# Cross attention with its running maxima in bf16, and their negatives spread by one product of a constant tile with placed tops

## The chip, the cores and the metric

The kernel runs on one core of one Trainium2 chip. The core's engines are TensorE (PE; its weight loads are shown apart as PEld), VectorE (DVE), ScalarE (ACT), GpSimd (POOL) and SyncE (SP, which only issues transfers here). Each engine works through its own list of instructions in order, and semaphores tie the lists together. The metric is the device time of one execution in microseconds; lower is better.

## The reference, cut to what matters

The program is a two-layer decoder on `x` of shape (4, 256, 256): self attention, memory attention and a ternary feed-forward network, then a gated scan, cross attention and a mixture of experts. The change lies in the cross attention of the second layer. Per batch row there are 256 queries in 16 heads of width 128 and 4 key/value heads, each shared by four query heads; the keys are the 256 own positions and 1601 context positions, 1857 in all:

```
q, k = rope(rms_norm(x @ Wq)), rope(rms_norm(own_and_context @ Wk))
p    = exp((q @ k.T - m) * 128**-0.5)      # m: one number per query and head, near the row's maximum
out  = (p @ v) / sum(p)                    # any m gives the same quotient; it guards against overflow
x   += out @ Wo
```

## The kernel before, in words

Scores are made transposed: keys on the partitions, queries along the free dimension. A **pass** h is one half (two heads x 256 queries = 512 columns) of one of the 16 groups (batch row, key/value head), so there are 32 passes (`PASSES`), two to a group; a pass with an even h is the first half of its group. Each pass has 15 **steps** (`STEPS`), one per tile of 128 keys (65 in the last). `cross_stream` writes the program of every engine by hand as a loop over **slots** (`SLOTS`), one step per slot: in slot s the functions are called that are due at s minus a fixed lag (`TOPS_LATE`, `LOWER`, `WEIGH` and so on). Nothing reorders this afterwards.

For one step: PE makes the scores (`score`, L1956, three bf16 products into bank 0 or 1), ACT copies them to SBUF (`copy_scores`, L2053), DVE takes the running maximum from the bank (`keep_most`, L2237 for the second step of a pass, L2240 for the rest), 18 slots later DVE adds the negative maximum (`lower`, L2226, which reads PSUM bank 7), ACT makes the exponent (L2059), POOL sums it up (L2168) and PE weighs the values (`weigh`, L1988). Beside this PE projects keys, values and queries for a later group (L1899), DVE rotates them (`rotate`, L2281 and L2282), POOL normalises them (L2175, L2181, L2186) and PE turns them (L1941); such a unit comes every five slots. `score` for step s waits until `keep_most` has read the bank at step s - 2.

At the end of a pass comes what is called a **turnover** here, numbered like its pass. The maximum over the partitions of `most` (128 x 512, f32) is taken and brought back to every partition:

- slot 15: `turn_most` (PE, L1964), four f32 transposes of `most` into bank 6
- slot 16: `take_top` (DVE, L2260), the maximum of each row, 128 x 4; `turn_top` (PE, L1970), a bf16 product that turns these to 4 x 128; `flatten` (ACT, L2101), the copy to SBUF as `flat` with its sign changed
- slot 17: `spread` (PE, L1977), four products of the rows of `own` (four rows of an identity, widened to 4 x 4 x 128) with `flat`, which put row c of `flat` on all partitions of bank 7. It waits for `flatten` and for the last `lower` of the pass before (65 x 512), which DVE does in slot 17
- slot 18: the first `lower` of the pass waits for `spread`

(slots counted from the pass's first.) `own` comes from an 8 x 8 constant that a transfer brings in at the start of the cross attention (L1663) and a DVE copy widens (L1695).

Of the kernel before, what the change touches and what calls it, by code (L numbers as in the profile page):

```python
# [8 lines left out]
ALU = mybir.AluOpType  # L9
# [9 lines left out]
P = 128  # L19
# [4 lines left out]
DC = DM // P  # L24
# [1559 lines left out]
TOPS_LATE, FLAT_LATE, SPREAD_LATE = STEPS, STEPS + 1, STEPS + 2  # L1584
# [49 lines left out]
def cross_attention(nc, x, const, a, w, kept, first_row, experts):  # L1634

    with Stage(nc, "cross") as keep:
# [6 lines left out]
        own8 = sb("own8", [8, 8])  # L1643
        own = sb("own", [4, 4, P], BF16)
# [6 lines left out]
        with Stage(nc, "cross_w") as st:  # L1651
# [5 lines left out]
            loaded, dve_step, rs_ready, rs_done, row_ready = (st.sem(s) for s in ("loaded", "dve_step", "rs_ready", "rs_done", "row_ready"))  # L1657
            row_t, own_hi = st.sem("row_t"), st.sem("own_hi")

            with nc.Block() as block:  # L1660
                @block.sync
                def _(sp):
# [27 lines left out]
                def _(ve):  # L1690
# [3 lines left out]
                    ve.wait_ge(loaded, 16)  # L1694
                    nc.vector.tensor_copy(own[:], bcast(own8[0:4, 0:4], 2, P))  # L1695
# [11 lines left out]
        cross_stream(nc, x, const, a, w, experts, w_q, w_kv, w_o, k_gain, q_gain, freq, ones, own, half, eps, own_t, in_t, ctx_t,  # L1707
# [3 lines left out]
def cross_stream(nc, x, const, a, w, experts, w_q, w_kv, w_o, k_gain, q_gain, freq, ones, own, half, eps, own_t, in_t, ctx_t,  # L1711
                 where, where_f, angle, turns, sin, k_tab, q_tab, raw):

    with Stage(nc, "stream") as st:
# [20 lines left out]
        flat = spare[0:4, DC * CTX - 128:DC * CTX - 64].bitcast(BF16)  # L1735
# [11 lines left out]
        most_turned, top_ready, top_turned, flat_ready, spread_ready = (  # L1747
            sem("most_turned"), sem("top_ready"), sem("top_turned"), sem("flat_ready"), sem("spread_ready"))
# [94 lines left out]
        for s in SLOTS:  # L1843
            for kind, items in (("tops", pass_at(s, TOPS_LATE)), ("flat", pass_at(s, FLAT_LATE)), ("turn", turns_in(s)),
                                ("sum", pass_at(s, SUM_LATE)), ("out", outs_in(s))):
                for item in items:
# [3 lines left out]
                    freed = {"tops": lambda: (top_ready, item + 1), "flat": lambda: (flat_ready, item + 1),  # L1850
# [3 lines left out]
        with nc.Block() as block:  # L1854
# [34 lines left out]
            def _(pe):  # L1889
# [131 lines left out]
                for slot in SLOTS:  # L2021
# [7 lines left out]
                    for h in pass_at(slot, FLAT_LATE):  # L2029
                        turn_top(h)  # L2030
# [706 lines left out]
```

## Time and profile before

| what | value |
| --- | --- |
| time, median of 3 runs | 1650.81 us (1650.22 to 1650.82) |
| profiled execution's own time | 1648.11 us |
| its span, first to last instruction | 1646.3 us |
| busy over the span: PE, DVE, ACT, POOL | 89%, 78%, 63%, 69% |
| granted TensorE clock, mean over the span | 0.966 |
| cross attention, steps and tail | from about 459 to 1567 us |

Busy shares are of the whole span and count neither register work nor waits. PE's busy time is modelled: a product of 512 columns is shown with 0.38 us, while the next one starts 0.21 to 0.22 us after it, so starts of consecutive PE rows say what a product costs and not their lengths. Consecutive DVE rows overlap too, by up to 0.09 us. A few PE records are missing.

### The profile page before, as it was taken

Reading aid. Unit: us, or ns where it says so; the run is one execution under the profiler, and the core shown is the slowest. Engines: PE = TensorE matmul, PEld = TensorE weight load, DVE = VectorE, ACT = ScalarE, POOL = GpSimd, SP = SyncE. Lnnn points to the kernel's source line nnn. Section 1 sums busy time; section 2 is a strip of 40 time slices with the busy share of each in tenths; the row PEclk is TensorE's granted clock in tenths of the full one; section 3 lists DMA queues with packets and bytes.
Section 4 is the critical chain, followed back from the end, with each engine's and each line's share of the span. In section 5 each row is a group of like instructions: output and inputs, shape, how many; then the busy total and the mean of one; then the engine's idle time right before and its main releaser. Section 6 shows DMA issues by size and latency. Waiting matters only on the chain. (4 is left out here: it accounts for less than half of the span.)

```text
span 1646.3 us, 25844 instructions
## 1 busy us (share of the span) xinstructions
PE 1470.2 (89%) x8223; PEld 855.8 (52%) x8332; DVE 1287.7 (78%) x2581; ACT 1029.3 (63%) x2439; POOL 1127.9 (69%) x1033
## 2 busy tenths in 40 slices
PE   6598697757778999999999999989999999999988
PEld 5477365533544555455455555545545555554455
DVE  7876577878569888787977888887887878878766
ACT  3364464744366777676677766676776766766552
POOL 2363471112459789988978998888898878877742
PEclk9799798979899999999999999999999999999999
DMA  3000831020000001000000100000000000000020
GB/s 102 1 2 2 296 114 39 1 73 0 32 1 14 14 1 41 14 1 1 1 1 1 28 14 1 1 1 1 14 28 1 1 1 1 1 1 1 1 59 26
DMA packets 30991, 38.47 MB, mean 23 GB/s; under 512 B 4996, under 2 KB 26504, under 8 KB 30856
## 3 DMA queue, kind: packets, MB, share of 16 engines
q1 hardware_dynamic: 30856, 36.82, 6.9%
q8 instruction: 67, 1.10, 0.3%
q14 instruction: 68, 0.56, 0.1%
HBM read 35.76 MB, written 1.05 MB: 22 GB/s over the span
## 5 line engine op out<-in xcount | busy, mean ns | idle before, releaser
L2168 POOL TENSOR_TENSOR stream_acc<-stream_acc,stream_weights 128x512 f32<-128x512 f32 (+1 forms) x374 | 491.9, 1315 | 80.6 <-ACT stream_weights L2059 59.0
L1988 PE MATMUL stream_banks<-stream_weights,stream_v 128*128 128x512 f32 (+1 forms) x876 | 451.6, 600 | 0.0
L2240 DVE TENSOR_TENSOR stream_most<-stream_most,stream_banks 128x512 f32<-128x512 f32 (+1 forms) x416 | 284.9, 685 | 157.4 <-ACT stream_weights L2053 142.2
L2053 ACT COPY stream_weights<-stream_banks 128x512 f32<-128x512 f32 (+1 forms) x438 | 256.6, 586 | 238.8 <-PE stream_banks L1956 231.0
L2059 ACT ACTIVATE stream_weights<-stream_weights 128x512 f32<-128x512 f32 (+1 forms) x438 | 278.5, 637 | 60.2 <-DVE stream_weights L2226 57.6
L2226 DVE TENSOR_TENSOR stream_weights<-stream_weights,stream_banks 128x512 f32<-128x512 f32 (+1 forms) x438 | 297.0, 680 | 2.8 <-PE stream_banks L1977 1.5
L2175 POOL TENSOR_TENSOR stream_by_cos<-stream_by_cos,stream_by_sin 128x256 f32<-128x256 f32 x192 | 135.8, 728 | 88.4 <-DVE stream_by_sin L2282 88.2
L1956 PE MATMUL stream_banks<-stream_q_t_lo,stream_k_t_hi 128*128 128x512 bf16 (+1 forms) x479 | 181.7, 379 | 9.2 <-DVE stream_most L2240 3.1
L1956 PE MATMUL stream_banks<-stream_q_t_hi,stream_k_t_lo 128*128 128x512 bf16 (+1 forms) x480 | 182.1, 379 | 0.1
L1956 PE MATMUL stream_banks<-stream_q_t_hi,stream_k_t_hi 128*128 128x512 bf16 (+1 forms) x388 | 147.6, 381 | 15.5 <-DVE stream_most L2240 14.8
L1988 PEld LDWEIGHTS stream_banks<-stream_weights,stream_v 128*128 128x128 f32 (+1 forms) x876 | 144.0, 191 | 29.7 <-issue 5.3
L1956 PEld LDWEIGHTS stream_banks<-stream_q_t_hi,stream_k_t_hi 128*128 128x128 bf16 (+1 forms) x480 | 47.2, 98 | 140.6 <-issue 99.0
L1956 PEld LDWEIGHTS stream_banks<-stream_q_t_lo,stream_k_t_hi 128*128 128x128 bf16 (+1 forms) x480 | 47.5, 99 | 134.7 <-issue 134.3
L2186 POOL TENSOR_TENSOR stream_normed<-stream_by_cos,row_ctx_t 128x512 f32<-128x512 f32 x96 | 96.8, 1008 | 8.4 <-PE stream_banks L1941 1.1
L2069 ACT ACTIVATE stream_squares<-stream_banks 128x128 bf16<-128x128 f32 x368 | 97.2, 278 | 8.1 <-PE stream_banks L1899 7.8
L2181 POOL TENSOR_TENSOR row_ctx_t<-row_ctx_t,cross_half 128x4 f32<-128x4 f32 x96 | 98.2, 1023 | 0.0
L1899 PE MATMUL stream_banks<-early_w_kv_hi,row_in_t_hi 128*128 128x256 bf16 x416 | 79.4, 273 | 5.0 <-DVE stream_by_sin L2282 5.0
L1899 PE MATMUL stream_banks<-early_w_kv_lo,row_in_t_hi 128*128 128x256 bf16 x416 | 79.4, 273 | 0.0
L1899 PE MATMUL stream_banks<-early_w_kv_hi,row_in_t_lo 128*128 128x256 bf16 x416 | 79.4, 273 | 0.0
L2069 ACT ACTIVATION_READ_ACCUMULATOR stream_squares<-stream_banks 128x1 f32 x368 | 77.1, 210 | 0.0
L1956 PEld LDWEIGHTS stream_banks<-stream_q_t_hi,stream_k_t_lo 128*128 128x128 bf16 (+1 forms) x480 | 47.4, 99 | 56.5 <-issue 0.3
L1899 PEld LDWEIGHTS stream_banks<-early_w_kv_hi,row_in_t_hi 128*128 128x128 bf16 x416 | 40.4, 98 | 51.8 <-DVE stream_by_sin L2282 6.0
(445 smaller groups left out, 3099.6 us busy)
## 6 DMA issues: line engine op xcount, KB each, us to landing
memory_raw_t<-in_ctx_t SPq DMA_DIRECT2D x4, 1601.0 KB, 9.1
memory_raw<-in_ctx SPq DMA_DIRECT2D x4, 1536.0 KB
row_ctx_t<-in_ctx_t SPq DMA_DIRECT2D x6, 512.0 KB, 3.7
early_raw<-in_L_xattn_Wq SPq DMA_DIRECT2D x4, 512.0 KB, 3.8
early_raw<-in_L_xattn_Wo SPq DMA_DIRECT2D x4, 512.0 KB, 3.9
row_ctx_t<-in_ctx_t SPq DMA_DIRECT2D x1, 1601.0 KB, 7.0
moe_raw_up<-in_L_ffn_wi SPq DMA_DIRECT2D x6, 256.0 KB, 4.3
model_x<-in_x SPq DMA_DIRECT2D x1, 1024.0 KB, 5.4
```

Source lines behind the costliest of these rows:

```text
L1899: last = nc.tensor.matmul(out, rows, moving(two, c), start=(n == 0), stop=(n == 3 * DC - 1))
L1956: last = nc.tensor.matmul(ps[0:r, step % 2, :], k_t[one][:, t * P:t * P + r], q_t[two][:, g % 2, PAIR * n:PAIR * (n + 1), :], start=(one = ...
L1988: nc.tensor.matmul(ps[:, 2 + n, :], v[0:r, g % 2, t, :], room(step)[0:r], start=(t == 0), stop=(t == KT - 1)).then_inc(weighed, 1)
L2053: nc.scalar.copy(room(step)[0:r], ps[0:r, step % 2, :]).then_inc(copied, 1)
L2059: nc.scalar.activation(room(step)[0:r], room(step)[0:r], ACT.Exp, scale=SCALE).then_inc(p_ready, 1)
L2069: last = nc.scalar.activation(squares[:, h, :], heads[:, h - some.start, :], ACT.Square, accum_out=ss[:, u % 2, h:h + 1])
L2168: nc.gpsimd.tensor_tensor(acc[0:r, h % 2, :], acc[0:r, h % 2, :], room(step)[0:r], ALU.add).then_inc(acc_ready, 1)
L2175: last = nc.gpsimd.tensor_tensor(by_cos[:, u % 2, 0:n, to], by_cos[:, u % 2, 0:n, to], by_sin[:, u % 2, 0:n, of], ALU.add)
L2181: nc.gpsimd.tensor_tensor(rms[:, u % 2, 0:n], var[:, u % 2, 0:n], half[:, 0:n], ALU.pow).then_inc(rms_ready, 1)
L2186: nc.gpsimd.tensor_tensor(normed[:, 0:n], by_cos[:, u % 2, 0:n], bcast(rms[:, u % 2, 0:n], 2, HD), ALU.mult).then_inc(normed_ready, 1)
L2226: nc.vector.tensor_tensor(room(step)[0:r], room(step)[0:r], ps[0:r, 7, :], ALU.add).then_inc(lowered, 1)
L2240: nc.vector.tensor_tensor(most[0:r], most[0:r], ps[0:r, step % 2, :], ALU.max).then_inc(maxed, 1)
```

## The change

`most` becomes bf16 (each running maximum is rounded), and `turn_most` transposes it as bf16 into the first half of bank 6, seen as bf16 (`turned_most`). `take_top` reads those. `turn_top` and `flatten` are gone. In their place DVE gets `place_top` in slot 16, after `take_top` and `lower` and ahead of `rotate`: it multiplies the bf16 identity with `top`, each read four times and 128 times over, which gives `tops`, four diagonal tiles of 128 x 128 with the tops on the diagonals. `spread` is then a single bf16 product of `less`, a constant 128 x 128 tile of -1.0, with the 512 columns of `tops`; every partition of bank 7 gets the negative tops. It waits for `place_top` instead of `flatten`. The constant's transfer and the copy that widened it are gone; POOL fills `less`.

```diff
         ones = sb("ones", [P, 1])
-        own8 = sb("own8", [8, 8])
-        own = sb("own", [4, 4, P], BF16)
+        less = sb("less", [P, P], BF16)
...
-                    sp.dma_start(own8[:], a["c_cross_own"]).then_inc(loaded, 16)
...
                     nc.gpsimd.memset(ones[:], 1.0)
+                    nc.gpsimd.memset(less[:], -1.0)
...
-                    ve.wait_ge(loaded, 16)
-                    nc.vector.tensor_copy(own[:], bcast(own8[0:4, 0:4], 2, P))
                     ve.wait_ge(rs_done, 1)
...
-        most = sb("most", [P, HALF])
+        most = sb("most", [P, HALF], BF16)
+        tops = sb("tops", [P, 4, P], BF16)
         top = sb("top", [P, 4], BF16)
...
+        turned_most = ps[:, 6, :].bitcast(BF16)[:, 0:HALF]
...
                     for c in range(4):
-                        last = nc.tensor.transpose(ps[:, 6, c * P:(c + 1) * P], most[:, c * P:(c + 1) * P], const["ident"][:])
+                        last = nc.tensor.transpose(turned_most[:, c * P:(c + 1) * P], most[:, c * P:(c + 1) * P], const["ident_b"][:])
                     last.then_inc(most_turned, 1)
 
-                def turn_top(h):
-                    pe.wait_ge(top_ready, h + 1)
-                    wait_bank6("flat", h)
-                    nc.tensor.matmul(ps[0:4, 6, 0:P], top[:], const["ident_b"][:], start=True, stop=True).then_inc(top_turned, 1)
-
                 def spread(h):
-                    pe.wait_ge(flat_ready, h + 1)
+                    pe.wait_ge(tops_ready, h + 1)
                     if h >= 1:
                         pe.wait_ge(lowered, STEPS * h)
-                    for c in range(4):
-                        last = nc.tensor.matmul(ps[:, 7, c * P:(c + 1) * P], own[:, c, :], flat, start=True, stop=True)
-                    last.then_inc(spread_ready, 1)
+                    nc.tensor.matmul(ps[:, 7, :], less[:], tops[:].rearrange("p c n -> p (c n)"), start=True, stop=True).then_inc(spread_ready, 1)
...
-                def flatten(h):
-                    ac.wait_ge(top_turned, h + 1)
-                    if h >= 1:
-                        ac.wait_ge(spread_ready, h)
-                    nc.scalar.mul(flat, ps[0:4, 6, 0:P], -1.0).then_inc(flat_ready, 1)
...
                 def take_top(h):
                     ve.wait_ge(most_turned, h + 1)
+                    nc.vector.tensor_reduce(top[:], turned_most.rearrange("p (c n) -> p c n", c=4), AX_X, ALU.max).then_inc(top_ready, 1)
+
+                def place_top(h):
+                    ve.wait_ge(top_ready, h + 1)
                     if h >= 1:
-                        ve.wait_ge(top_turned, h)
-                    nc.vector.tensor_reduce(top[:], ps[:, 6, :].rearrange("p (c n) -> p c n", c=4), AX_X, ALU.max).then_inc(top_ready, 1)
+                        ve.wait_ge(spread_ready, h)
+                    nc.vector.tensor_tensor(tops[:], bcast(const["ident_b"][:], 1, 4), bcast(top[:], 2, P), ALU.mult).then_inc(tops_ready, 1)
...
                     if 0 <= slot - LOWER < ALL:
                         lower(slot - LOWER)
+                    for h in pass_at(slot, TOPS_LATE + 1):
+                        place_top(h)
```

On TensorE, from the last projection of slot 15 to the scores of slot 18 at turnover 2, before (line numbers are those of each kernel's own file; L1964 turns the maxima, L1988 weighs, L1956 makes scores, L1970 turns the tops, L1977 spreads):

```order
L1964 MATMUL stream_banks<-model_ident,stream_most 128x128 x4
L1988 MATMUL stream_banks<-stream_weights,stream_v 128x512
L1956 MATMUL stream_banks<-stream_q_t_hi,stream_k_t_hi 128x512
L1956 MATMUL stream_banks<-stream_q_t_lo,stream_k_t_hi 128x512
L1956 MATMUL stream_banks<-stream_q_t_hi,stream_k_t_lo 128x512
L1899 MATMUL stream_banks<-early_w_kv_hi,row_in_t_hi 128x256 x2
L1899 MATMUL stream_banks<-early_w_kv_lo,row_in_t_hi 128x256 x2
L1899 MATMUL stream_banks<-early_w_kv_hi,row_in_t_lo 128x256 x2
L1970 MATMUL stream_banks<-model_ident_b,stream_top 4x128
L1988 MATMUL stream_banks<-stream_weights,stream_v 128x512
...
L1988 MATMUL stream_banks<-stream_weights,stream_v 128x512
L1977 MATMUL stream_banks<-row_ctx_t,cross_own 128x128 x4
```

And the same stretch now:

```order
L1958 MATMUL stream_banks<-model_ident_b,stream_most 128x128 x4
L1975 MATMUL stream_banks<-stream_weights,stream_v 128x512
L1950 MATMUL stream_banks<-stream_q_t_hi,stream_k_t_hi 128x512
L1950 MATMUL stream_banks<-stream_q_t_lo,stream_k_t_hi 128x512
L1950 MATMUL stream_banks<-stream_q_t_hi,stream_k_t_lo 128x512
L1893 MATMUL stream_banks<-early_w_kv_hi,row_in_t_hi 128x256 x2
L1893 MATMUL stream_banks<-early_w_kv_lo,row_in_t_hi 128x256 x2
L1893 MATMUL stream_banks<-early_w_kv_hi,row_in_t_lo 128x256 x2
L1975 MATMUL stream_banks<-stream_weights,stream_v 128x512
...
L1975 MATMUL stream_banks<-stream_weights,stream_v 128x512
L1965 MATMUL stream_banks<-stream_tops,cross_less 128x512
```

The small product between the projections and the second `weigh` is gone, and the last four products are one.

On VectorE, from `take_top` to the maximum of slot 17 at the same turnover, before:

```order
L2260 TENSOR_REDUCE stream_top<-stream_banks 128x4
L2226 TENSOR_TENSOR stream_weights<-stream_weights,stream_banks 128x512
L2281 TENSOR_TENSOR stream_by_cos<-stream_banks,row_k_tab_cos 128x256
L2282 TENSOR_TENSOR stream_by_sin<-stream_banks,row_k_tab_sin 128x256
L2237 TENSOR_TENSOR stream_most<-stream_weights,stream_banks 128x512
L2226 TENSOR_TENSOR stream_weights<-stream_weights,stream_banks 65x512
L2240 TENSOR_TENSOR stream_most<-stream_most,stream_banks 128x512
```

And now:

```order
L2235 TENSOR_REDUCE stream_top<-stream_banks 128x4
L2203 TENSOR_TENSOR stream_weights<-stream_weights,stream_banks 128x512
L2241 TENSOR_TENSOR stream_tops<-model_ident_b,stream_top 128x512
L2262 TENSOR_TENSOR stream_by_cos<-stream_banks,row_k_tab_cos 128x256
L2263 TENSOR_TENSOR stream_by_sin<-stream_banks,row_k_tab_sin 128x256
L2214 TENSOR_TENSOR stream_most<-stream_weights,stream_banks 128x512
L2203 TENSOR_TENSOR stream_weights<-stream_weights,stream_banks 65x512
L2217 TENSOR_TENSOR stream_most<-stream_most,stream_banks 128x512
```

`place_top` (L2241) stands ahead of four instructions, the last of which, `lower` on 65 partitions, is the one that `spread` on TensorE waits for.

## Rows read from the trace of the kernel before

**Rows 1.** Window: busy us of PE, PEld, DVE, ACT, POOL; then granted clock, DMA
```profile
1300.00:1400.00 100.00, 99.42 (x496) 54.80 (x502) 79.49 (x146) 68.69 (x194) 82.57 (x78) 1.00 0.00 1
```

**Rows 2.** Timeline, TensorE, turnover 15 and slots behind it: start, length, instruction
```profile
1003.61 0.60 PE L1964 MATMUL stream_banks<-model_ident,stream_most 128*128 128x128 f32 x4
1004.05 1.02 PE L1988 MATMUL stream_banks<-stream_weights,stream_v 128*128 128x512 f32 x2
...
1005.34 0.38 PE L1956 MATMUL stream_banks<-stream_q_t_hi,stream_k_t_lo 128*128 128x512 bf16 x1
...
1006.98 0.38 PE L1956 MATMUL stream_banks<-stream_q_t_lo,stream_k_t_hi 128*128 128x512 bf16 x1
1007.20 0.38 PE L1956 MATMUL stream_banks<-stream_q_t_hi,stream_k_t_lo 128*128 128x512 bf16 x1
...
1008.37 0.39 PE L1977 MATMUL stream_banks<-row_ctx_t,cross_own 4*128 4x128 bf16 x4
1008.92 0.38 PE L1956 MATMUL stream_banks<-stream_q_t_lo,stream_k_t_hi 128*128 128x512 bf16 x1 [0.16 <-DVE stream_most L2240]
...
1013.88 0.38 PE L1956 MATMUL stream_banks<-stream_q_t_hi,stream_k_t_lo 128*128 128x512 bf16 x1
...
1015.17 0.38 PE L1956 MATMUL stream_banks<-stream_q_t_lo,stream_k_t_hi 128*128 128x512 bf16 x1
```

**Rows 3.** Timeline, TensorE, memory attention: products of 65 columns
```profile
197.74 0.23 PE L862 MATMUL memory_banks<-memory_ctx_t_hi,memory_xn_t_hi 128*128 128x65 bf16 x2
197.80 0.22 PE L862 MATMUL memory_banks<-memory_ctx_t_lo,memory_xn_t_hi 128*128 128x65 bf16 x2
```

**Rows 4.** Timeline, VectorE, turnover 15
```profile
1004.25 0.69 DVE L2260 TENSOR_REDUCE stream_top<-stream_banks 128x4 bf16<-128x512 f32 x1 [1.02 <-PE stream_banks L1964]
1004.86 0.68 DVE L2226 TENSOR_TENSOR stream_weights<-stream_weights,stream_banks 128x512 f32<-128x512 f32 x1
1005.45 0.42 DVE L2281 TENSOR_TENSOR stream_by_cos<-stream_banks,row_k_tab_cos 128x256 f32<-128x256 f32 x1
1005.79 0.42 DVE L2282 TENSOR_TENSOR stream_by_sin<-stream_banks,row_k_tab_sin 128x256 f32<-128x256 f32 x1
1006.38 0.69 DVE L2237 TENSOR_TENSOR stream_most<-row_ctx_t,stream_banks 128x512 f32<-128x512 f32 x1 [0.17 <-ACT row_ctx_t L2053]
1006.98 0.68 DVE L2226 TENSOR_TENSOR stream_weights<-stream_weights,stream_banks 65x512 f32<-65x512 f32 x1
```

**Rows 5.** Timeline, last lowering and spread at turnover 14
```profile
971.78 0.68 DVE L2226 TENSOR_TENSOR stream_weights<-stream_weights,stream_banks 65x512 f32<-65x512 f32 x1
...
973.82 0.39 PE L1977 MATMUL stream_banks<-row_ctx_t,cross_own 4*128 4x128 bf16 x4
```

**Rows 6.** Timeline, the same pair at turnover 17
```profile
1076.87 0.68 DVE L2226 TENSOR_TENSOR stream_weights<-stream_weights,stream_banks 65x512 f32<-65x512 f32 x1
...
1077.70 0.38 PE L1977 MATMUL stream_banks<-row_ctx_t,cross_own 4*128 4x128 bf16 x4 [1.45 <-DVE stream_weights L2226]
```

**Rows 7.** Groups by line and shape, VectorE: count, busy us, mean ns
```profile
L2286 DVE TENSOR_TENSOR stream_k_t_lo<-stream_banks,stream_k_t_hi 128x512 bf16<-128x512 f32 x48 | 32.9, 686 | 6.7 <-ACT stream_k_t_hi L2095 6.7
L1023 DVE TENSOR_TENSOR ffn_tern_proj<-ffn_tern_proj,ffn_below 128x2048 f16<-128x2048 f16 x1 | 1.2, 1224 | 0.0
```

**Rows 8.** Line L2346, both inputs in SBUF: ns minimum/median/maximum
```profile
L2346 DVE TENSOR_TENSOR cross_w_o_lo<-early_raw,cross_w_o_hi x8: 685/1045/1693, 485.6 to 708.3; 128x512 bf16<-128x512 f32 x8
```

**Rows 9.** Timeline, GpSimd at three places, VectorE with two SBUF inputs beside it
```profile
1004.72 1.03 POOL L2181 TENSOR_TENSOR row_ctx_t<-row_ctx_t,cross_half 128x4 f32<-128x4 f32 x1
...
516.00 1.02 POOL L2181 TENSOR_TENSOR row_ctx_t<-row_ctx_t,cross_half 128x4 f32<-128x4 f32 x1
516.04 1.17 DVE L2358 SCALAR_TENSOR_TENSOR early_angle<-cross_turns,early_angle 128x960 f32<-128x960 f32 x1
...
1508.02 1.26 POOL L2168 TENSOR_TENSOR stream_acc<-stream_acc,stream_weights 128x512 f32<-128x512 f32 x1 [1.02 <-ACT stream_weights L2059]
1508.04 1.78 DVE L2341 TENSOR_TENSOR row_in_t_lo<-row_ctx_t,row_in_t_hi 128x512 bf16<-128x512 f32 x1
```

More of the change, by code:

```diff
@@ L1581, in pass_at @@
     return [h] if rest == 0 and 0 <= h < PASSES else []
-TOPS_LATE, FLAT_LATE, SPREAD_LATE = STEPS, STEPS + 1, STEPS + 2
+TOPS_LATE, SPREAD_LATE = STEPS, STEPS + 2
 ATT_LATE = STEPS + WEIGH
@@ L1656, in cross_attention @@
             rs = st.sb("rs", [P, 3, TILES])
-            loaded, dve_step, rs_ready, rs_done, row_ready = (st.sem(s) for s in ("loaded", "dve_step", "rs_ready", "rs_done", "row_ready"))
+            dve_step, rs_ready, rs_done, row_ready = (st.sem(s) for s in ("dve_step", "rs_ready", "rs_done", "row_ready"))
             row_t, own_hi = st.sem("row_t"), st.sem("own_hi")
             with nc.Block() as block:
-                @block.sync
-                def _(sp):
-                    sp.dma_start(own8[:], a["c_cross_own"]).then_inc(loaded, 16)
                 @block.gpsimd
@@ L1705, in _, with cross_stream @@
                                                 own_t[0][:, :, tok], ALU.subtract)
-        cross_stream(nc, x, const, a, w, experts, w_q, w_kv, w_o, k_gain, q_gain, freq, ones, own, half, eps, own_t, in_t, ctx_t,
+        cross_stream(nc, x, const, a, w, experts, w_q, w_kv, w_o, k_gain, q_gain, freq, ones, less, half, eps, own_t, in_t, ctx_t,
                      where, where_f, angle, turns, sin, k_tab, q_tab, kept["raw"])
-def cross_stream(nc, x, const, a, w, experts, w_q, w_kv, w_o, k_gain, q_gain, freq, ones, own, half, eps, own_t, in_t, ctx_t,
+def cross_stream(nc, x, const, a, w, experts, w_q, w_kv, w_o, k_gain, q_gain, freq, ones, less, half, eps, own_t, in_t, ctx_t,
                  where, where_f, angle, turns, sin, k_tab, q_tab, raw):
@@ L1746, in cross_stream @@
         scored, copied, maxed, lowered = sem("scored"), sem("copied"), sem("maxed"), sem("lowered")
-        most_turned, top_ready, top_turned, flat_ready, spread_ready = (
-            sem("most_turned"), sem("top_ready"), sem("top_turned"), sem("flat_ready"), sem("spread_ready"))
+        most_turned, top_ready, tops_ready, spread_ready = sem("most_turned"), sem("top_ready"), sem("tops_ready"), sem("spread_ready")
         p_ready, acc_ready, weighed = sem("p_ready"), sem("acc_ready"), sem("weighed")
@@ L1843, in cross_stream @@
         for s in SLOTS:
-            for kind, items in (("tops", pass_at(s, TOPS_LATE)), ("flat", pass_at(s, FLAT_LATE)), ("turn", turns_in(s)),
+            for kind, items in (("tops", pass_at(s, TOPS_LATE)), ("turn", turns_in(s)),
                                 ("sum", pass_at(s, SUM_LATE)), ("out", outs_in(s))):
@@ L1849, in cross_stream @@
                     bank6_before[kind, item] = freed
-                    freed = {"tops": lambda: (top_ready, item + 1), "flat": lambda: (flat_ready, item + 1),
+                    freed = {"tops": lambda: (top_ready, item + 1),
                              "turn": lambda: (lo_ready, item + 1), "sum": lambda: (inv_ready, item + 1),
@@ L2028, in _ @@
                         turn_most(h)
-                    for h in pass_at(slot, FLAT_LATE):
-                        turn_top(h)
                     for u in turns_in(slot):
@@ L2126, in _ @@
                             vary(u, 1)
-                    for h in pass_at(slot, FLAT_LATE):
-                        flatten(h)
                     for u in turns_in(slot):
@@ L2691, in constants @@
     c["c_cross_freq"] = (1.0 / np.float32(10000.0) ** (np.arange(0, P, 2, dtype=np.float32) / np.float32(P))).astype(np.float32)
-    c["c_cross_own"] = np.eye(8, dtype=np.float32)
     return c
```

1 line of the change is left out of this document (removed).

## The prediction

> **What bounds the kernel now.** I read the busy shares first, then windows of 100 us over the cross attention, then the timeline of TensorE around the turnovers, and last that of VectorE there. In a window of the stream TensorE is busy 99.4 of 100 us at a granted clock of 1.00, VectorE 79, ScalarE 69, GpSimd 83 [rows 1]. TensorE's busy time is modelled, so I checked it by the starts: a slot with nothing but scores and one weighing takes 1.29 us from the third score product to the second of the next slot, which is six products of 512 columns at 0.215 us [rows 2]. So it really is back to back, and work taken off TensorE in the stream is worth its length, unless the engine then runs into a wait. The nearest such wait is in the turnover itself: `spread` waits for the `lower` on 65 partitions. At odd turnovers that ends 1008.37 - (1006.98 + 0.68) = 0.71 us before `spread` starts [rows 2, 4], at even ones 1.36 us [rows 5]. Where VectorE is the later one the gap is 0.15 us, which is what the semaphore costs [rows 6]. Fifteen even turnovers (0 to 28) are of the second kind, nine odd ones (3, 7, 11, 15, 19, 23, 25, 27, 29) of the first. Eight are not regular: 1, 9 and 17 (VectorE busy with the angles of the next row, TensorE held), 5, 13 and 21 (parts of the next context) and the last two.
>
> **TensorE's side.** The four transposes take 1004.05 - 1003.61 = 0.44 us. In bf16 I take 512 columns at the pace of a bf16 product, 0.215 us, so 0.22 less. No bf16 product of 128 columns with a full tile load stands alone in this trace; products of 65 columns, each with such a load, start 0.03 us apart [rows 3], so the load does not stand in the way of 0.054 us each. The other end is that nothing is gained. `turn_top` goes: from the third score product to the second of the next slot it is 1006.98 - 1005.34 = 1.64 us with it and 1.29 us without, so 0.35 us; its 128 columns alone would be 0.054, the rest are pauses around it. `spread` costs 1008.92 - 1007.20 - 1.29 = 0.43 us as four products and I expect 0.215 us as one full-size product of 512 columns, so 0.21 less [rows 2]. Together 0.78 us a turnover, of which 0.57 us lies before `spread`.
>
> The Trainium skill (TensorE: Matmul & The Clock Gate, Back-to-back issue gap) gives about 81 ns for a sustained pair of load and product at 128 columns. By that the transposes would take 0.32 us and not 0.215, and 24 turnovers would bring 2.5 us less. The rows of 65 columns speak against a floor that high here.
>
> **VectorE's side.** The new `keep_most` reads bf16 from SBUF and f32 from PSUM and writes bf16; L2286 has exactly these operands and takes 686 ns [rows 7], as long as the maximum before (0.69 us, [rows 4]). `take_top` reads as many elements. Neither moves. `place_top` is added: 512 elements, both inputs in SBUF, bf16. Bounds: 0.42 us if two elements pass per cycle (L1023, all 16 bit, 2048 elements in 1224 ns, so 0.52 us less for each thousand elements fewer, [rows 7]); 0.69 us when nothing is in its way and up to 1.69 us [rows 8]. I take the 0.69, in which 0.60 us passes until the next start, since `top` is one element read 128 times over and not a row of neighbours.
>
> The rest is a wait w for GpSimd. L2341 started 0.02 us behind a sum on GpSimd and ended 0.54 us after that sum did; L2358, started 0.04 us behind the short L2181, was not held (960 elements in 1.17 us) [rows 9]. So w is what is left of a sum, a rotation sum (L2175) or a normalisation at that moment, less 0.13 us. I looked at what GpSimd does at 1.63 us behind the transposes, where `place_top` would start. At turnover 15 that is 1005.24, in the middle of L2181 (1004.72 to 1005.75, [rows 9]), and so at nearly all regular odd turnovers; w is nothing as beside L2358 or, if L2181 holds the port after all, 0.51 - 0.13 = 0.38 us: I take 0.18. At the even ones it falls on the end of L2181 or w is 0.25 to 0.5 us.
>
> The Trainium skill (SBUF — State Buffer, Who interferes with whom) has it stricter: a VectorE instruction with two SBUF inputs and a GpSimd instruction that reads SBUF exclude each other for the whole instruction. By that w would be 0.38 us at the nine odd turnovers, and the sum 1.8 us smaller; the row of L2358 does not bear that out for L2181, that of L2341 does for a sum.
>
> **Turnover 15, step by step.** `take_top` starts 0.22 us earlier, at 1004.03; `lower` 1004.64, `place_top` 1005.24, the rotations 1005.84 and 1006.18 (they stood at 1005.45 and 1005.79), the maximum 1006.51 without its former wait of 0.17 us for the copy, `lower` on 65 partitions 1007.11 to 1007.79, all plus w. That is 0.13 + w later than before [rows 4]. TensorE is ready for `spread` at 1008.37 - 0.57 = 1007.80 and gets it at 1007.79 + w + 0.15, so it waits 0.14 + w. An odd turnover gains 0.78 - 0.14 - 0.18 = 0.46 us. At an even one 1.36 - 0.15 - 0.57 - 0.13 = 0.51 us is left for w, so the whole 0.78 us comes through. Behind `spread` nothing is late: the maximum of slot 17 and the next lowering have waits of more than half a microsecond ahead of them, and the score product that needs them comes two slots on. GpSimd's own delay (up to 0.7 us) is covered by the two slots between normalising and turning.
>
> At 1, 9 and 17 VectorE sets the time, so nothing saved on TensorE counts and `place_top` adds 0.60 + w, 0.8 us each with 0.18 [rows 6]. For 5, 13, 21 and the last two, where VectorE is late but not always, I take half, 0.4 us lost each.
>
> The copy of the constant and its transfer stood beside ScalarE's root, on which the next step waits anyway: nothing. `flatten` leaves ScalarE, which waits for TensorE's scores behind it: nothing.
>
> **The sum.** 15 x 0.78 = 11.7, 9 x 0.46 = 4.1, less 3 x 0.8 and 5 x 0.4 = 4.4: 11.4 us less, 1648.1 - 11.4 = 1636.7 us for the profiled execution. The median of the runs stands 2.7 us above the profiled time, so 1639.4 us for the median; I say 1639.
>
> **Rivals.** (1) The port makes it slower. With w = 1.0 us at each turnover, as in the worst rows of L2346 [rows 8], an even turnover gains 0.78 - 0.49 = 0.29, an odd one loses 0.36, turnovers 1, 9, 17 lose 1.6 and the other five 1.2 each: 4.4 - 3.2 - 4.8 - 6.0 = 9.6 us slower, 1660. Gain and loss balance at a mean w of about 0.7. For it: GpSimd is busy 83% here and L2346 waited 0.36 us on average. Against: the start falls beside the short L2181 most times. (2) `place_top` is quick, 0.42 us, or never waits: the odd turnovers come to 0.7 and the irregular ones lose half as much; 15 x 0.78 + 9 x 0.7 - 2.2 = 16 us, 1635. (3) The transposes gain nothing in bf16: TensorE and VectorE both lose the 0.22 us at 24 turnovers, 5 us, 1644. (4) The gain is eaten: w near 0.6 everywhere, or waits of ScalarE and GpSimd behind TensorE take back what the turnovers give; within 0.2% (3.3 us, about what a measurement of this kernel can tell from no change), 1648 to 1654.
>
> **Chances.** The forecast (1636 to 1642) 0.45; (2) with still less lost at the irregular turnovers (1630 to 1636) 0.2; (3) or a loss of like size (1642 to 1647.5) 0.15; (4) 0.12; (1) 0.08. Range 1631 to 1648: the low end is 15 x 0.78 + 9 x 0.78 with nothing lost elsewhere, 19 us, the high end leaves out (1) and most of (4). Faster 0.80, same 0.12, slower 0.08.
>
> **What would show it.** Right: the transposes start 0.05 to 0.06 us apart and `place_top` lasts 0.69 us; the distance between transposes of regular passes shrinks from 32.1 and 35.2 us to about 31.5 and 34.5; TensorE waits at odd turnovers for L2203 on 65 partitions by 0.1 to 0.4 us and at even ones not at all; 1, 9 and 17 grow. Wrong: `place_top` at a mean over 1.2 us; transposes still 0.11 us apart; the maximum in bf16 longer than 0.69 us; or a new wait ahead of the scores in the rest of the pass, which would say that TensorE was not the only bound.

## The result and the profile after

The changed kernel takes 1640.3 us (median, 1639.1 to 1641.5), the kernel before 1650.8 on the same chip: a ratio of 0.9937, 95% interval 0.992 to 0.9955. The forecast was 1639, in a range of 1631 to 1648. The profiled execution took 1639.1 us, with this span and granted clock (0.966 before):

```profile
core 0: 1637.1 us, clock 0.962
```

The window of rows 1 in the changed kernel. PE is busy 99.98 of 100 us, DVE 83 (79 before), POOL 84:

```profile
1300.00:1400.00 100.00, 99.98 (x507) 55.54 (x505) 83.26 (x155) 69.03 (x190) 83.90 (x79) 1.00 0.00 1
```

Turnover 15 on the timeline, PE, DVE and POOL together, with the columns of rows 2 and 4 (L1958 transposes, L2235 is `take_top`, L2241 `place_top`, L2203 `lower`, L1965 `spread`; L2158 the square root, L2163 the normalisation):

```profile
1000.79 0.39 PE L1958 MATMUL stream_banks<-model_ident_b,stream_most 128*128 128x128 bf16 x4
1001.02 1.08 PE L1975 MATMUL stream_banks<-stream_weights,stream_v 128*128 128x512 f32 x2
1001.22 0.69 DVE L2235 TENSOR_REDUCE stream_top<-stream_banks 128x4 bf16<-128x512 bf16 x1 [0.82 <-PE stream_banks L1958]
...
1001.88 1.03 POOL L2158 TENSOR_TENSOR row_ctx_t<-row_ctx_t,cross_half 128x4 f32<-128x4 f32 x1
...
1002.36 0.38 PE L1950 MATMUL stream_banks<-stream_q_t_hi,stream_k_t_lo 128*128 128x512 bf16 x1
1002.42 0.69 DVE L2241 TENSOR_TENSOR stream_tops<-model_ident_b,stream_top 128x512 bf16<-128x512 bf16 x1
...
1003.65 0.38 PE L1950 MATMUL stream_banks<-stream_q_t_lo,stream_k_t_hi 128*128 128x512 bf16 x1
...
1004.28 0.68 DVE L2203 TENSOR_TENSOR stream_weights<-stream_weights,stream_banks 65x512 f32<-65x512 f32 x1
...
1005.10 0.38 PE L1965 MATMUL stream_banks<-stream_tops,cross_less 128*128 128x512 bf16 x1
1005.32 0.38 PE L1950 MATMUL stream_banks<-stream_q_t_hi,stream_k_t_hi 128*128 128x512 bf16 x1
```

The transposes take 0.23 us for 0.44 (the weighing behind them gives 0.05 back), third score product to second of the next slot 1003.65 - 1002.36 = 1.29 us for 1.64, `spread` 0.22 for 0.43. `lower` on 65 partitions ends at 1004.96 and `spread` starts at 1005.10: it now waits for it, where 0.71 us was to spare [rows 2, 4]. From one regular turnover's transposes to the next one's it is now 31.55 and 34.48 us, where it was 32.12 and 35.20: the signs that the forecast named for being right.

For all turnovers I took the distance from one turnover's transposes to the next one's in both traces. The table has what each group of turnovers gained in us, first to last, for the changed kernel and for the experiments e1 to e10 of the next section (e11 is the changed kernel once more), between turnovers 0 and 31 (in the profile of before 481.50 to 1538.65, so 1057.15 us apart; after 1047.15). This distance is the better gauge: what lies ahead of it differs from one execution to the next (turnover 0 begins at 480.5 to 486.9 us in the profiles of this study). It is still one execution of each kernel, and behind equal gaps at 9 and 17 the granted clock fell in some of these executions and not in others, so a difference in those three columns is not by itself the edit's.

| kernel | 15 even | 9 odd | 1 | 9 | 17 | 5, 13, 21, 30 | sum |
| --- | --- | --- | --- | --- | --- | --- | --- |
| forecast | 11.7 | 4.1 | -0.8 | -0.8 | -0.8 | -1.6 | 11.8 |
| changed kernel | 9.43 | 5.14 | -1.04 | -1.14 | -1.14 | -1.25 | 10.00 |
| changed kernel again, e11 | 9.43 | 5.10 | -1.05 | -1.16 | -1.16 | -1.28 | 9.88 |
| e1 bf16 alone | 2.48 | 1.48 | 0.06 | 0.02 | 0.03 | 0.31 | 4.38 |
| e2 placing alone | 4.55 | 3.18 | -1.06 | -0.55 | 0.00 | -1.44 | 4.68 |
| e3 placed twice | -5.51 | -7.44 | -1.07 | -2.27 | -4.00 | -4.29 | -24.58 |
| e4 on ScalarE | 8.11 | 3.03 | -0.65 | -0.05 | -1.22 | -0.56 | 8.66 |
| e5 spread later | 9.57 | 6.56 | 0.12 | 0.02 | 0.02 | -1.15 | 15.14 |
| e6 both of these | 9.03 | 6.53 | -0.63 | -0.05 | -0.04 | 0.13 | 14.97 |
| e7 tops in PSUM | 9.48 | 5.15 | -0.52 | 0.01 | 0.02 | 0.24 | 14.38 |
| e8 e7 and e5 | 9.50 | 6.53 | -0.53 | 0.02 | 0.01 | 0.39 | 15.92 |
| e9 f32 tops in SBUF | 9.34 | 5.08 | -1.66 | -0.56 | 0.00 | -1.36 | 10.84 |
| e10 gap filled | 9.39 | 5.07 | 0.09 | -0.01 | -0.01 | -1.37 | 13.16 |

### The profile page after: what moved, and what is told of

Its sections match the earlier page's. It is cut to its first block and busy times, and to the rows that moved or that the text cites. A ratio compares the mean times of both kernels' runs of the same rounds, so it can differ in the third digit from the quotient of the medians.

```text
span 1637.1 us, 25648 instructions
## 1 busy us (share of the span) xinstructions
PE 1462.8 (89%) x8204; PEld 847.8 (52%) x8204; DVE 1305.8 (80%) x2612; ACT 1022.6 (62%) x2407; POOL 1133.5 (69%) x1034
## 3 DMA queue, kind: packets, MB, share of 16 engines
HBM read 35.76 MB, written 1.05 MB: 22 GB/s over the span
## 5 line engine op out<-in xcount | busy, mean ns | idle before, releaser
L2217 DVE TENSOR_TENSOR stream_most<-stream_most,stream_banks 128x512 bf16<-128x512 bf16 (+1 forms) x416 | 284.7, 684 | 138.4 <-ACT stream_weights L2038 124.0
L2203 DVE TENSOR_TENSOR stream_weights<-stream_weights,stream_banks 128x512 f32<-128x512 f32 (+1 forms) x438 | 296.8, 680 | 1.9 <-PE stream_banks L1965 0.6
L1950 PE MATMUL stream_banks<-stream_q_t_hi,stream_k_t_hi 128*128 128x512 bf16 (+1 forms) x480 | 183.1, 381 | 15.4 <-DVE stream_most L2217 13.9
L2163 POOL TENSOR_TENSOR stream_normed<-stream_by_cos,row_ctx_t 128x512 f32<-128x512 f32 x96 | 100.1, 1043 | 8.4 <-PE stream_banks L1935 1.1
L2158 POOL TENSOR_TENSOR row_ctx_t<-row_ctx_t,cross_half 128x4 f32<-128x4 f32 x96 | 100.4, 1046 | 0.0
```

What stands on the lines that cost most here:

```text
L1950: last = nc.tensor.matmul(ps[0:r, step % 2, :], k_t[one][:, t * P:t * P + r], q_t[two][:, g % 2, PAIR * n:PAIR * (n + 1), :], start=(one = ...
L2158: nc.gpsimd.tensor_tensor(rms[:, u % 2, 0:n], var[:, u % 2, 0:n], half[:, 0:n], ALU.pow).then_inc(rms_ready, 1)
L2163: nc.gpsimd.tensor_tensor(normed[:, 0:n], by_cos[:, u % 2, 0:n], bcast(rms[:, u % 2, 0:n], 2, HD), ALU.mult).then_inc(normed_ready, 1)
L2203: nc.vector.tensor_tensor(room(step)[0:r], room(step)[0:r], ps[0:r, 7, :], ALU.add).then_inc(lowered, 1)
L2217: nc.vector.tensor_tensor(most[0:r], most[0:r], ps[0:r, step % 2, :], ALU.max).then_inc(maxed, 1)
```

## The experiments

**The two parts apart.** e1 is the kernel before with bf16 maxima and bf16 transposes and nothing else:

```diff
-        most = sb("most", [P, HALF])
+        most = sb("most", [P, HALF], BF16)
```

> The kernel before with the maxima in bf16 alone; turn_top, flatten and the four spreading products stay. Theory (what a turnover saves is TensorE's issue time, as far as VectorE's chain in front of the spread does not hold it): the transposes and the weighing behind them take 0.16 us less at some 26 turnovers, none of it lost in a wait, so 4 us less than before, 1646.5 us. Rival (bf16 transposes bring nothing of their own; all comes from the products that went away): 1650.5 us.

Measured 1646.7 us, before 1649.6, ratio 0.998 (0.9971 to 0.9989). It gains 0.16 us at most regular turnovers and next to nothing where VectorE leads (0.02 to 0.06 at 1, 9 and 17). So rival (3) is out, and its other half is the 0.05 us of the weighing:

```profile
1003.43 0.39 PE L1965 MATMUL stream_banks<-model_ident_b,stream_most 128*128 128x128 bf16 x4
1003.66 1.08 PE L1989 MATMUL stream_banks<-stream_weights,stream_v 128*128 128x512 f32 x2
```

e2 is the changed kernel with f32 maxima and f32 transposes again. The wider `most` left no room for `less`, so that lies in spare columns there, GpSimd fills it inside the stream, and `spread` waits for that too:

```diff
-        most = sb("most", [P, HALF], BF16)
+        most = sb("most", [P, HALF])
```

> The changed kernel with the maxima and their transposes in f32 again. Theory: 0.16 us more at 26 turnovers, and take_top 0.22 us later while TensorE comes 0.22 us later too, so the wait ahead of the spread stays 0.15 us at odd turnovers: 1644.5 us. Rival (the bf16 part is worth nothing): 1640.5 us. Rival (the port wait of the placing hangs on its exact start, which moves by 0.22 us here): another 2 to 5 us on top, 1647 to 1650, with placings over 1 us long at the even turnovers.

Measured 1647.3 us, ratio 0.9978 (0.9968 to 0.9987): the second rival. Transposes 0.22 us longer put `place_top` (here L2242) 0.22 us later, and at turnovers 4, 8, 12, 16, 20, 24 and 26 that is just behind the start of the normalisation (L2164):

```profile
1039.91 1.04 POOL L2164 TENSOR_TENSOR stream_normed<-stream_by_cos,row_ctx_t 128x512 f32<-128x512 f32 x1
1040.04 1.45 DVE L2242 TENSOR_TENSOR stream_tops<-model_ident_b,stream_top 128x512 bf16<-128x512 bf16 x1
```

It ends 0.54 us behind the normalisation, as L2341 did behind a sum [rows 9]. In the changed kernel `place_top` comes first at the same turnover (16), and GpSimd is held instead, 1.52 us for 1.04:

```profile
1033.96 0.68 DVE L2241 TENSOR_TENSOR stream_tops<-model_ident_b,stream_top 128x512 bf16<-128x512 bf16 x1
1034.03 1.52 POOL L2163 TENSOR_TENSOR stream_normed<-stream_by_cos,row_ctx_t 128x512 f32<-128x512 f32 x1
```

At the 24 regular turnovers the bf16 maxima are thus worth 3.96 us alone and 14.57 - 7.73 = 6.84 with the placing: they also set who comes first. (The whole stretches say 4.38 and 5.3, but at turnover 17 of e2 the clock did not fall, and at 9 it fell later.)

**The placing doubled** (each copy with its own wait):

```diff
+                    nc.vector.tensor_tensor(tops[:], bcast(const["ident_b"][:], 1, 4), bcast(top[:], 2, P), ALU.mult).then_inc(tops_twice, 1)
+                    ve.wait_ge(tops_twice, h + 1)
                     nc.vector.tensor_tensor(tops[:], bcast(const["ident_b"][:], 1, 4), bcast(top[:], 2, P), ALU.mult).then_inc(tops_ready, 1)
```

> The changed kernel with the placing done twice over, the second time behind a wait for the first, about 0.7 to 0.75 us more on VectorE at each turnover. Theory: at odd turnovers TensorE already waits for VectorE, so 9 x 0.75; at the eight irregular ones 0.75 each; at even ones 0.5 us is spare, so 0.25 each, and 0.75 at 2, 10 and 18: 6.8 + 6 + 2.8 + 2.3 = 18 us more, 1658 us. Rival (the placing is hidden, and what the irregular turnovers lost has another cause): at most 2 us more, 1642 us.

Measured 1678.2 us, ratio 1.0176 (1.0163 to 1.019). The sign is as expected, the size was missed by 20 us, since the second copy starts beside the normalisation and is held. At turnover 15:

```profile
1018.02 1.03 POOL L2158 TENSOR_TENSOR row_ctx_t<-row_ctx_t,cross_half 128x4 f32<-128x4 f32 x1
1018.56 0.69 DVE L2241 TENSOR_TENSOR stream_tops<-model_ident_b,stream_top 128x512 bf16<-128x512 bf16 x1
1019.13 1.04 POOL L2163 TENSOR_TENSOR stream_normed<-stream_by_cos,row_ctx_t 128x512 f32<-128x512 f32 x1
1019.28 1.44 DVE L2243 TENSOR_TENSOR stream_tops<-model_ident_b,stream_top 128x512 bf16<-128x512 bf16 x1
```

The first copy, beside the square root on 4 elements, isn't held. Turnover 25 tells the two costs apart: there neither copy is held (0.69 us each), and it loses 0.73 us against the changed kernel, the 0.75 expected, where the other odd ones lose 1.48. VectorE's chain ahead of the 65-row `lower` is the bound of the odd turnovers.

**The placing on ScalarE**, as four scaled copies ahead of the copy of slot 16's scores:

```diff
+                    for c in range(4):
+                        last = nc.scalar.activation(tops[:, c, :], const["ident_b"][:], ACT.Copy, scale=top[:, c:c + 1])
```

> The changed kernel with the placing on ScalarE, four copies of 128 columns scaled by the top, ahead of the copy of the scores in slot 16. Theory (VectorE's 0.6 us is what the odd and the irregular turnovers lose): the odd ones gain 0.15 us each, turnovers 1, 5, 9, 13, 17 and 21 about 1.1 us each: 8 us less than the changed kernel, 1632 us. Rival (the loss at the irregular turnovers is GpSimd held off the port, or moves to ScalarE, whose copy of the scores comes 0.3 us or more later): 1637 to 1642 us.

Measured 1642.4 us, ratio 0.9946 (0.9931 to 0.9962): the rival, 0.4 us beyond its range. The odd turnovers gain 0.33 us each and not 0.57:

```profile
1006.50 1.30 ACT L2087 ACTIVATE stream_tops<-model_ident_b,stream_top 128x128 bf16<-128x128 bf16 x4
1007.68 0.59 ACT L2038 COPY row_ctx_t<-stream_banks 128x512 f32<-128x512 f32 x1
1008.30 0.69 DVE L2224 TENSOR_TENSOR stream_most<-row_ctx_t,stream_banks 128x512 bf16<-128x512 f32 x1 [0.72 <-ACT row_ctx_t L2038]
...
1009.73 0.38 PE L1965 MATMUL stream_banks<-stream_tops,cross_less 128*128 128x512 bf16 x1 [0.23 <-DVE stream_weights L2213]
```

The four copies (1.30 us) hold up the copy of the scores, that the maximum (0.72 us), that the `lower` behind it, and that `spread`: VectorE lost one instruction and gained a wait.

**Spread later**, behind the scores of slot 18:

```diff
-                    for h in pass_at(slot, SPREAD_LATE):
-                        spread(h)
                     if 0 <= slot < ALL:
                         score(slot)
+                    for h in pass_at(slot, SPREAD_LATE + 1):
+                        spread(h)
```

> The changed kernel with one thing moved: the product that spreads the negatives is issued behind the scores of slot 18 and no longer ahead of them, so TensorE has 0.65 us of score products to run while VectorE finishes the 65-row addition of slot 17 that frees bank 7. If TensorE's wait for that addition is what the odd turnovers (0.15 us each) and the irregular ones (0.5 to 1.5 us each, as far as 0.65 covers them) lose, the distance from the first turnover's transposes to the last one's is 3 to 5 us shorter than in the changed kernel, and the time is about 1636 to 1638 us against 1640. Rival: the next addition on VectorE then waits for the later product instead, the exponent and the weighing behind it are late by the same 0.65 us, and the even turnovers, which had no wait, lose what the odd ones gain: 1640 to 1645 us.

Measured 1636.1 us, ratio 0.9922 (0.9905 to 0.9939). The odd turnovers gain 0.73 us each, the whole of TensorE's saving, the even ones keep theirs, and 1, 9 and 17 are back at what they were before or better. With the scores issued first, the one long gap of turnover 9 (2.46 us in the changed kernel) is two of 0.81 and 1.05 us, and the granted clock stays at 1.00 there and at 17. Its first rows of PE's waits over 480 to 1550 us (total, times, longest), then the row of the changed kernel:

```profile
PE stream_banks L1950 <- DVE stream_most L2217: 12.2, 15, 1.3
...
PE stream_banks L1965 <- DVE stream_weights L2203: 4.7, 4, 1.7
```

```profile
PE stream_banks L1965 <- DVE stream_weights L2203: 12.7, 7, 4.0
```

> Placing on ScalarE (four scaled copies, as in the run with that alone, 1642.4 us) and the spreading product behind the scores of slot 18. On ScalarE the irregular turnovers lost less and the odd ones 0.23 us in front of the spreading product, since the four copies delay the copy of the scores, then the maximum, then the 65-row addition. If the later product hides that wait, each regular turnover keeps 0.5 to 0.7 us and the first-to-last distance is 3 to 5 us shorter than with the placing on ScalarE alone: 1636 to 1638 us. Rival: with ScalarE's copies late, the exponents are late too and the next pass waits for them: 1642 us or more.

e6 (ScalarE and later) measured 1636.1 us, ratio 0.9915 (0.99 to 0.9929), with the first-to-last distance 6.3 us shorter than e4's: more than the 3 to 5 expected, since turnover 17 gained another 1.2 (the clock fell there in e4 and not in e6).

**The maxima in PSUM:**

```diff
-        top = sb("top", [P, 4], BF16)
+        top = ps[:, 6, HALF - 4:HALF]
...
-                    freed = {"tops": lambda: (top_ready, item + 1),
+                    freed = {"tops": lambda: (tops_ready, item + 1),
```

> The changed kernel with the four maxima of a row kept in f32 in the last four columns of the transposes' own PSUM bank (the bf16 transposes fill only half of it), so that the placing multiplication reads one operand from PSUM, like every other element-wise VectorE operation of the pass, and the bank comes free behind the placing and not behind the maximum. Theory: VectorE and GpSimd shut each other out only when VectorE's operation has all its operands in SBUF. Then the placing takes 0.68 us in every turnover (now 0.68 to 1.81), GpSimd's square root, normalisation and sums beside it are not held, turnovers 1, 9, 13, 17 and 21 get back 0.3 to 1 us each, and the time is 2 to 3 us under the changed kernel's: about 1638 us. Rival: the placing is held wherever GpSimd runs, whatever it reads (durations up to 1.8 us again), and the later release of the bank delays the transposes of the next unit: 1640 to 1643 us.

Measured 1635.3 us, ratio 0.991 (0.9892 to 0.9928); the changed kernel had 0.9937 and 0.993, with intervals that overlap this one. Minimum, median and maximum of `place_top` in ns, in the changed kernel, in e7, and in e9, where the maxima are f32 but in SBUF:

```profile
L2241 DVE TENSOR_TENSOR stream_tops<-model_ident_b,stream_top x32: 678/685/1812, 483.0 to 1530.7; 128x512 bf16<-128x512 bf16 x32
```

```profile
L2241 DVE TENSOR_TENSOR stream_tops<-model_ident_b,stream_banks x32: 676/680/690, 481.7 to 1525.0; 128x512 bf16<-128x512 bf16 x32
```

```profile
L2241 DVE TENSOR_TENSOR stream_tops<-model_ident_b,stream_top x32: 680/686/1818, 481.7 to 1528.6; 128x512 bf16<-128x512 bf16 x32
```

And turnover 16 of e7, the place where GpSimd was held above:

```profile
1030.03 0.68 DVE L2241 TENSOR_TENSOR stream_tops<-model_ident_b,stream_banks 128x512 bf16<-128x512 bf16 x1
1030.10 1.04 POOL L2163 TENSOR_TENSOR stream_normed<-stream_by_cos,row_ctx_t 128x512 f32<-128x512 f32 x1
```

Not all of the 4.4 us of distance (14.38 against 10.00) belongs to PSUM. At turnovers 9 and 17 `place_top` takes 0.68 us in both kernels and nothing is held beside it, so its operand has nothing to do there; those two gained 2.3 us because the clock did not fall in this execution, behind gaps as long as in the changed kernel (2.69 us up to the scores, less the 0.22 of `spread`, whose row is missing). Here is turnover 9 with the 3 us behind it, where the changed kernel had a clock of 0.50:

```profile
795.39 0.38 PE L1950 MATMUL stream_banks<-stream_q_t_hi,stream_k_t_hi 128*128 128x512 bf16 x1 [2.69 <-DVE stream_weights L2203]
```

```profile
795.39:798.39 3.00, 3.00 (x14) 1.00 0.01 3
```

The other 2.1 us, at 1, 5, 13 and 21 above all, are where an instruction was held in the changed kernel and isn't now.

> The changed kernel with the four maxima of a row in f32 in SBUF, and nothing else: the placing multiplication then reads a bf16 and an f32 tile, both from SBUF, and writes bf16 to SBUF. It tells apart two reasons for which the placing is held while GpSimd works (0.68 to 1.81 us) and is not when the maxima lie in PSUM (0.68 us in all 32). Theory: what counts is where the operands lie; with both in SBUF it is held as in the changed kernel, 0.68, 0.89, 1.22 and 1.81 us in the same turnovers, and the time is the changed kernel's, 1640 us. Rival: what counts is that all three tiles are 16 bits wide; mixed with f32 it takes 0.68 us everywhere, as with PSUM, and the time is about 1636 us.

Measured 1639.5 us, ratio 0.9934 (0.9921 to 0.9948), with the lengths of the changed kernel. So the width isn't it: what counts is that one operand lies in PSUM, and then neither engine holds the other. e9's longer distance at turnover 1 (-1.66) is a clock that stayed at 0.50 for longer there, its smaller losses at 9 and 17 a clock that fell later (9) or not at all (17).

> Both of the last two moves: maxima in PSUM and the spreading product behind the scores of slot 18. If both work for their own reasons they add up, since one acts on GpSimd's delay in the irregular turnovers and the other on TensorE's wait for the 65-row addition: 1634 to 1636 us. If they act on the same waits, it is no faster than the better of the two: about 1637 us. If the later product only moves the wait to VectorE, it is as slow as that kernel, 1640 us or more.

e8 measured 1632.9 us, ratio 0.9898 (0.9882 to 0.9913), the fastest version found and 16 us under before on its chip. The two moves add up only in part, 15.92 us against 15.14 and 14.38: in both 9 and 17 are cured already, and turnover 1 stays at -0.53, as in e7, where e5 had 0.12. There a later angle instruction on VectorE (L2343, 0.67 us in the changed kernel) takes 3.15 us in e8 and 2.73 in e7, as its like took 3.15 in the kernel before.

**The gap filled** with products that nobody reads:

```diff
                     pe.wait_ge(tops_ready, h + 1)
+                    for _ in range({1: 24, 9: 12, 17: 12}.get(h, 0)):
+                        nc.tensor.matmul(ps[:, 6, HALF - 2 * P:HALF], less[:], tops[:, 0:2, :].rearrange("p c n -> p (c n)"), start=True, stop=True)
```

> The changed kernel with products whose results nobody reads in front of the spreading product's wait for the 65-row addition: 12 of 256 columns at turnovers 9 and 17, 24 at turnover 1, into the unused half of the transposes' bank (the outputs are the reference's). In the changed kernel TensorE stands idle for 4.02 us in turnover 1 and 2.46 us in 9 and 17, and in the 3 us behind each gap its granted clock is 0.50 and three score products take 1.28 us and not 0.65. Theory: the long idle stretch brings the clock down, and that costs turnovers 9 and 17 1.15 us each and turnover 1 about as much; with 1.3 to 2.6 us of the gap filled the granted clock stays 1.00 behind it, turnovers 9 and 17 come out even with before (-1.14 now) and the time is 3 to 3.5 us under the changed kernel's, 1636 to 1637 us. Rival: the clock falls for another reason or falls all the same; 1640 us, or more if the filling delays the spreading product.

> The changed kernel itself, unaltered, so that the two others of this call have their own comparison on the same chip: 1640 us, 0.9937 of before. If its first-to-last distance differs from the first profile's by more than 0.3 us, the clock's falls behind turnovers 1, 9 and 17 are not the same in every execution, and that difference is worth 1.15 us for each.

e10 measured 1638.1 us, ratio 0.9922 (0.9909 to 0.9936), the changed kernel again (e11) 1640.5, ratio 0.993 (0.9917 to 0.9944). The median of e10 is 1 us above what was expected, and the intervals overlap; the distances show where the difference lies: 13.16 us against 9.88, all of it at 1, 9 and 17 (e11 itself is within 0.12 us of the first execution of the changed kernel). Turnover 9 in the changed kernel, windows of 1 us of PE alone (length, busy time, granted clock, DMA share, GB/s), then two of its timeline rows:

```profile
795.56:796.56 1.00, 0.00 (x0) 1.00 0.00 0
796.56:797.56 1.00, 0.22 (x1) 0.73 0.00 0
797.56:798.56 1.00, 1.00 (x3) 0.50 0.00 0
798.56:799.56 1.00, 1.00 (x4) 0.50 0.03 8
799.56:800.56 1.00, 1.00 (x5) 0.57 0.00 0
```

```profile
797.34 0.58 PE L1965 MATMUL stream_banks<-stream_tops,cross_less 128*128 128x512 bf16 x1 [2.46 <-DVE stream_weights L2203]
...
798.57 0.63 PE L1950 MATMUL stream_banks<-stream_q_t_hi,stream_k_t_lo 128*128 128x512 bf16 x1
```

And in e10:

```profile
794.28 1.47 PE L1964 MATMUL stream_banks<-stream_tops,cross_less 128*128 128x256 bf16 x12
796.83 0.39 PE L1967 MATMUL stream_banks<-stream_tops,cross_less 128*128 128x512 bf16 x1 [1.07 <-DVE stream_weights L2205]
797.05 0.38 PE L1950 MATMUL stream_banks<-stream_q_t_hi,stream_k_t_hi 128*128 128x512 bf16 x1
```

Behind 2.46 us of idling the products run at half the clock, 0.42 us apart, for some 3 us; with 1.07 us left they come 0.22 apart, and the turnover is 1.15 us shorter (37.26 for 38.41 in e11). The clock fell at 1, 9 and 17 in both executions of the changed kernel and at none of the three here, so the filling is the likely reason; but gaps of 2.47 us went without a fall in e7 and e9, and one execution of e10 doesn't prove it.

Nor are the slow products all of the 1.15 us. They make ScalarE's copy of the scores late, VectorE waits 0.28 us for it, and its third angle instruction (960 elements, both inputs in SBUF) starts 9.90 us behind the transposes and not 9.54. There it falls into a sum on GpSimd and is held. In the changed kernel, then in e10:

```profile
800.46 1.95 DVE L2341 SCALAR_TENSOR_TENSOR early_angle<-cross_turns,early_angle 128x960 f32<-128x960 f32 x1
```

```profile
799.67 1.15 DVE L2343 SCALAR_TENSOR_TENSOR early_angle<-cross_turns,early_angle 128x960 f32<-128x960 f32 x1
```

0.36 later and 0.80 longer is 1.16. In e9 and e2 the clock fell at turnover 9 too, but this instruction took 1.15 us, and the turnover lost 0.55.

## Why the forecast came out, step by step

- **What bounds the kernel**: right. Work taken off TensorE came through wherever VectorE was not later: 0.70 to 0.73 us at most even turnovers.
- **TensorE's three savings**: `turn_top` 0.35 and `spread` 0.22 as forecast. The transposes' 0.22 was mis-sized, 0.16 net, since the weighing behind them costs 0.05 more (e1): 0.06 at each of twelve even turnovers, 0.7 us less in all.
- **`place_top` and w, its wait for GpSimd**: the 0.69 us was right, and the mean w of 0.18 too high at the odd turnovers, where it falls beside the square root and w is 0. They gained 0.57 and not 0.46 each, 1 us more in all. At 2, 10 and 18 w is 0.54, at 6, 14 and 22 0.2, within the spare time or little over it (2, 10 and 18 gain 0.69 to 0.70) and near the 0.25 to 0.5 that was computed.
- **All 15 even turnovers keep all**: wrong for three. Turnovers 12 and 20 gain 0.28 us, and 0.24 to 0.29 in every kernel with bf16 maxima and one placing, on whichever engine; 0 gains 0.29, which together is 1.5 us less. At 12 and 20 the slots ahead of the next turnover end on VectorE's rotation (a wait of 0.25 us in the trace), which is a part of what is missing; nothing was tried on that.
- **1, 9 and 17 lose 0.8 each**: the size was near, by luck, and the reason wrong. `place_top` isn't held at 9 and 17, and its own 0.60 us isn't lost either: without the clock's fall both come out even (e5, e7, e10, and 17 in e2 and e9). VectorE had a wait there that the forecast did not see. Before, its angle instruction starts inside a normalisation and takes 1.75 us; `place_top` moves it 0.60 us later, to 0.13 us before the normalisation's end, and it takes 1.15. The 65-row `lower` starts 5.95 us behind the transposes where it was 5.94. Turnover 9, before and then changed:

```profile
796.83 1.04 POOL L2186 TENSOR_TENSOR stream_normed<-stream_by_cos,row_ctx_t 128x512 f32<-128x512 f32 x1
797.14 1.75 DVE L2358 SCALAR_TENSOR_TENSOR early_angle<-cross_turns,early_angle 128x960 f32<-128x960 f32 x1
```

```profile
794.41 1.04 POOL L2163 TENSOR_TENSOR stream_normed<-stream_by_cos,row_ctx_t 128x512 f32<-128x512 f32 x1
795.32 1.15 DVE L2341 SCALAR_TENSOR_TENSOR early_angle<-cross_turns,early_angle 128x960 f32<-128x960 f32 x1
```

  What they lost instead, 1.14 each, came by another way: the products that used to lie in TensorE's wait were gone, the gap grew from 1.46 to 2.46 us, the clock fell, and the third angle instruction was held. Turnover 1 is a sum of more: `place_top` is held there (1.81 us), the 65-row `lower` comes 2.4 us later, a later angle instruction takes 0.67 us where it took 3.15, and with the gap filled it comes out even (e10). The forecast asked what is late, not how long TensorE then stands still, nor which waits of VectorE the later start takes away.
- **"GpSimd's own delay is covered by the two slots"**: wrong at 13 and 21. There `place_top` starts beside the first rotation sum, the pair of sums takes 1.97 us for 1.42, the normalisation comes later, and TensorE waits 0.98 us for it:

```profile
932.65 1.97 POOL L2152 TENSOR_TENSOR stream_by_cos<-stream_by_cos,stream_by_sin 128x256 f32<-128x256 f32 x2
932.67 0.68 DVE L2241 TENSOR_TENSOR stream_tops<-model_ident_b,stream_top 128x512 bf16<-128x512 bf16 x1
...
938.00 0.66 PE L1935 MATMUL stream_banks<-model_ident,stream_normed 128*128 128x128 f32 x4 [0.98 <-POOL stream_normed L2163]
```

  With the maxima in PSUM these lose 0.18 and 0.16 us, not 0.74 and 0.72 (e7), so the mutual hold was the larger part.
- **5, 13, 21 and the last two lose 0.4 each**: near in sum alone. 5 lost 0.44 and 13 and 21 lost 0.73 each where 0.4 was forecast, and 30 gained 0.65.
- **The sum**: 11.8 us forecast for the stretch and 10.00 measured. The even turnovers brought 2.3 less, the odd ones 1.0 more, the irregular ones 0.6 less. The span shrank by 9.2: turnover 0 came 0.4 us later (the first TensorE instruction came 0.3 later), and the tail lost another 0.4, with `place_top` 1.44 us long at turnover 31. For the profiled execution the forecast was 1636.7 and 1639.1 was measured, 2.4 off in 11.4. The median came out 1.3 us from the forecast because it stood 1.2 us above the profiled execution and not 2.7, so part of that closeness is luck, as is the clock, which makes 3.4 us here and behind gaps of one length fell or not.
- **Rivals**: (2) is half true, as it never waits at the odd turnovers; (1) and (4) name a real mechanism, which e2 and e3 show at work once the start moves by 0.22 us.

## What to carry to other kernels

When an added VectorE operation runs beside GpSimd, let it read one operand from PSUM if a few columns are free there: that took away both engines' waits and was worth 2 us of distance here. An instruction that is put ahead of others also moves those: at turnovers 9 and 17 one of them left a wait by it, and the added 0.60 us cost nothing. When work is taken out of an engine's gap, look where the consumer can be issued later (moving one product behind three others gave the most, 5 us of distance, 3.5 of it at the three turnovers with the long gap), and see how long TensorE then stands idle, since behind gaps of over 2 us it often ran at half its clock here. And check the start of the added operation against the other engine's timeline to 0.1 us: which one comes first decided here who waited.

## What the runs showed of the hardware that was not expected

- VectorE's 512-element multiplication with both operands in SBUF and GpSimd's element-wise operations shut each other out, and the one that started first went first. Started 0.13 us behind a normalisation it ended 0.54 us after it (e2); started 0.07 us ahead it took 0.68 us and the normalisation 1.52 instead of 1.04. A multiplication that starts inside GpSimd's square root of 4 elements (1.03 us) isn't held, but a square root that starts behind one is (1.46 us at turnover 2, 1.02 in e7). With an operand in PSUM neither is held at all (e7), and the width of the maxima doesn't matter (e9).
- The granted clock fell to 0.50 for about 3 us behind gaps of 2.46 and 4.02 us on TensorE, in both profiles of the changed kernel, and at turnover 1 also behind 2.20 us (e7) and behind two gaps of 1.46 and 1.74 us (e5). In e9 it stayed down for some 5 us behind 4.07 us. Gaps of the same 2.47 us left it at 1.00 at turnovers 9 and 17 of e7 and 17 of e9, so a gap of that length may go either way; what decides was not found. The kernel before had a fall too, behind 1.98 us at turnover 5, and it cost nothing: the turnover is 36.86 us long, and 36.87 in e1, which had no fall. Behind the 0.94 and 1.07 us that e10 left it was 1.00 each time.
- bf16 transposes of 128 x 128 start 0.056 us apart (the changed kernel, four in a row), and bf16 products of 256 columns 0.109 us apart (e10, twelve in a row).
